# Causal attention: the last norm's statistics of one sequence moved behind the last row maximum, and the copies of each group's outputs moved from VectorE to ScalarE

## The reference, cut to what matters

```python
h = _layernorm(x, ln1_w, ln1_b)          # then a causal convolution of three taps over the rows
q, k, v = jnp.split(h @ attn_w, 3, axis=-1)   # 16 heads of 8, rotated
scores = jnp.where(causal, q @ k.T / jnp.sqrt(D), -1e30)
y = jax.nn.softmax(scores, axis=-1) @ v
x = x + y @ proj_w
h = _layernorm(x, ln2_w, ln2_b)
expert_idx = jnp.argmax(h @ router_w, axis=-1)     # one of 4 experts for each row
x = x + chosen expert of h (gate * sigmoid(gate) * value @ expert_proj)
```

## Time and profile before

| what | us |
|---|---|
| median of 3 runs | 343.56 (342.61 to 343.8) |
| the profiled execution | 344.2, its span 342.4 |
| TensorE, VectorE, ScalarE, GpSimd busy | 317.1, 248.9, 216.5, 127.7 |
| attention loop in the profile | about 107 to 187 |
| L900, the copies, 8 on VectorE | 119.4 to 186.9, 0.68 each |

### The profile page before, as it was taken

The page is one execution under the profiler, slowest core; times in us unless marked ns, Lnnn a source line. Parts: engine busy times, 40 slices in busy tenths (PEclk is TensorE's granted clock), DMA queues, the critical chain, the costliest instruction groups (busy, mean ns, idle before and its releaser), DMA issues.

```text
span 342.4 us, 6803 instructions
## 1 busy us (share of the span) xinstructions
PE 317.1 (93%) x2270; PEld 221.3 (65%) x2270; DVE 248.9 (73%) x766; ACT 216.5 (63%) x641; POOL 127.7 (37%) x183
## 2 busy tenths in 40 slices
PE   8799989998989999997999998998999899999886
PEld 2348778664544333354544998995678687878675
DVE  4988875884889999988352563379787867888476
ACT  1488885374466755564378664764776576676995
POOL 3455563110732444403231360410685525545400
PEclk9999999999999999998799999999999999999999
DMA  7590000086752520090002003100100000000002
GB/s 210 192 278 5 2 0 2 9 264 173 208 190 72 138 74 3 11 351 15 2 17 71 2 23 101 50 0 0 56 17 17 1 2 0 3 0 0 2 0 64
DMA packets 21881, 22.47 MB, mean 66 GB/s; under 512 B 3894, under 2 KB 18646, under 8 KB 21846
## 3 DMA queue, kind: packets, MB, share of 16 engines
q1 hardware_dynamic: 18982, 16.78, 17.0%
q10 hardware_dynamic: 2352, 4.20, 3.8%
q0 software_dynamic: 512, 1.05, 1.0%
HBM read 14.22 MB, written 7.60 MB: 64 GB/s over the span
## 4 chain that ended last, share of the span: by engine, by line
PE 57%; DVE 17%; ACT 13%; issue 5%; POOL 4%; DMA 3%; SPq 0%; ACTq 0%; POOLq 0%
PE PS L1388 51%; PE PS L1442 5%; DVE PS L873 5%; ACT big L1176 5%; ACT big L1364 3%; POOL big L529 2%; DVE big L691 2%; DMA big<-in_A_WkT 2%; DVE big L716 2%; ACT big L1306 1%; DMA XN<-scr_y,pos 1%; ACT big L1150 1%; DVE XN L668 1%; POOL big L531 1%; DVE mraw L705 1%
## 5 line engine op out<-in xcount | busy, mean ns | idle before, releaser
L1388 PE MATMUL PS<-big 128*128 128x128 f32 (+10 forms) x592 | 94.6, 311 | 9.1 <-DVE mB L873 4.1
L1388 PEld LDWEIGHTS PS<-big 128*128 128x128 f32 (+3 forms) x592 | 56.4, 151 | 42.9 <-DVE mB L873 21.3
L529 POOL TENSOR_TENSOR big<-big,urec 128x1024 f32<-128x1024 f32 x24 | 45.6, 1898 | 60.2 <-DVE urec L723 45.5
L1176 ACT ACTIVATE big<-big 128x154 f32<-128x154 f32 x192 | 60.5, 318 | 10.9 <-DVE big L691 5.6
L873 DVE CUSTOM_DVE_ANT_0 PS<-PS,later 128x128 f32<-128x128 f32 (+3 forms) x128 | 59.9, 516 | 8.8 <-PE PS L1388 7.6
L1306 ACT ACTIVATE big<-PS 128x1024 f32<-128x1024 f32 (+3 forms) x64 | 42.8, 701 | 31.1 <-PE PS L1388 31.1
L1150 ACT ACTIVATE big<-PS 128x1280 f32<-128x1280 f32 (+2 forms) x30 | 32.3, 1087 | 27.0 <-PE PS L1442 24.5
L1388 PE MATMUL PS<-kkC,XT 128*128 128x462 f32 (+1 forms) x96 | 36.0, 511 | 2.2 <-DVE big L716 2.2
L517 POOL TENSOR_TENSOR rstd<-ve,minus_half 128x4 f32<-128x4 f32 (+2 forms) x13 | 13.2, 1016 | 61.8 <-DVE ve L663 61.8
L1176 ACT ACTIVATION_READ_ACCUMULATOR big<-big 128x1 f32 x192 | 36.1, 188 | 0.0
L1388 PEld LDWEIGHTS PS<-vwCm,big 128*128 128x128 f32 x256 | 30.9, 192 | 3.9 <-ACT big L1150 1.3
(11 more groups left out here) (193 smaller groups left out, 507.0 us busy)
## 6 DMA issues: line engine op xcount, KB each, us to landing
scr_qk<-big SPq DMA_DIRECT2D x12, 384.0 KB, 3.3
big<-scr_qk SPq DMA_DIRECT2D x16, 288.0 KB
big<-in_wv ACTq DMA_DIRECT2D x1, 2048.0 KB, 8.0
scr_x<-zrow SPq DMA_DIRECT2D x2, 448.0 KB, 6.4
scr_y<-big SPq DMA_DIRECT2D x2, 448.0 KB, 3.5
X<-in_x ACTq DMA_DIRECT2D x2, 256.0 KB, 3.4
big<-in_A_WoT ACTq DMA_DIRECT2D x1, 512.0 KB, 4.7
cw<-in_C_Wk SPq DMA_DIRECT2D x1, 512.0 KB, 5.3
```

The source lines that it names most:

```text
L529: pool.tensor_tensor(pn[:, 0:GH * P].rearrange("p (h k) -> p h k", h=GH), Pt[u % 3][:, :, 0:KM], r.to_broadcast([P, GH, KM]), ALU.mult).th ...
L1176: i = act.activation(Pt[u % 3][:, h, :], Pt[u % 3][:, h, :], ACT.Exp, accum_out=usum[:, u % 3, h:h + 1])
L1388: return pe.matmul(o, lhsT, rhs, start=start, stop=stop)
```

## The change

Four edits. On VectorE, `ln_m(0)` moves from step 20 to step 22, behind the last three maxima; `add_attention(0)` stays in step 20. On GpSimd, `split_maxima(7)` moves from behind `apply_m(0)` to before the root of that norm. `copy_outputs` leaves VectorE, with its waits, and stands in ScalarE's loop before the first exponential of the same steps (5, 9, ... 29). The last one, `copy_outputs(1, 3)`, stands behind ScalarE's loop, before `slots_out`. What is computed is the same.

```diff
@@ GpSimd
             split_maxima(6)
+            split_maxima(7)
...
             for b in range(B):
                 ln_rsqrt("m", (b,))
                 apply_m(b)
-                if b == 0:
-                    split_maxima(7)
                 pool.wait_ge(ln_norm["m"], QT * b + QT)
                 scatter(b)
@@ VectorE
-            def copy_outputs(b, g):
-                dve.wait_ge(av_step, QT * (4 * b + g + 1))
-                if b:
-                    dve.wait_ge(y_turned, g + 1)
-                dve.tensor_copy(yg[:, g, :], PS[:, AV_BANK, :]).then_inc(yg_ready, 1)
-
...
             for s in range(2 * 16):
                 g = (s - 5) // QT
-                if s % QT == 1 and s >= 5:
-                    copy_outputs(*divmod(g, 4))
                 if s < M_STEPS:
                     ring_maximum(3 * s)
...
                 elif s == S_TAIL + 2:
                     add_attention(0)
+                elif s == M_STEPS:
                     ln_m(0)
                 elif s == S_TAIL + 5:
                     route(0)
...
-            copy_outputs(1, 3)
             normalise_group(1, 3)
@@ ScalarE
+            def copy_outputs(b, g):
+                act.wait_ge(av_step, QT * (4 * b + g + 1))
+                if b:
+                    act.wait_ge(y_turned, g + 1)
+                copy(yg[:, g, :], PS[:, AV_BANK, :]).then_inc(yg_ready, 1)
+
             for n in range(B * 4 * QT * 2):
                 s, pair = divmod(n, 2)
+                if not pair and s % QT == 1 and s >= 5:
+                    copy_outputs(*divmod((s - 5) // QT, 4))
                 w = T - P * (s % QT)
                 act.wait_ge(st_mm, n + 1)
...
+            copy_outputs(1, 3)
             for part in range(len(SLOT_PARTS)):
                 slots_out(0, part)
```

## The result

The changed kernel takes **340.18 us** in the median of 6 runs (339.01 to 340.81); the kernel before, beside it, takes 343.69 (342.61 to 344.07, 6 runs). The ratio is **0.9899**, 95% interval [0.9872, 0.9926]. Forecast were 338.6 and a range of 336.7 to 341.0. Faster was right and the range holds the time, but the gain is 3.5 us and not 5. All medians and ranges here are of all executions, while the ratios and their intervals leave out the few that lie 1.5% or more above the fastest of the same kernel. The profiled executions give 344.2 and 340.81, with spans of 342.35 and 338.63, so 3.7 us of the gain can be followed in the two traces.

The account below looks back on a forecast made before the run. TensorE was taken to bound the kernel, through its waits in the attention loop and a clock dip. Terms -0.45 - 5.0 + 0.05 + 0.45 = -4.95 took the profiled 344.2 to 339.25, median 338.6; range 336.7 to 341.0.

Parts of the forecast that it names:

- The statistics moved: Steps 20 to 22: VectorE takes the next maximum earlier, TensorE's 2.15 us stall goes and its clock stays full; gain 5.0.
- the ring: Steps 5, 9, 13, 17: without VectorE's copy, output products start when GpSimd's mask ends, 0.13 earlier; gain 0.45 in all.
- Rival (a): Attention loop: maxima, not TensorE's last product, set the group, so four copies give 2.4 instead of 0.45; 336.7, chance 0.10.
- Step 29: ScalarE's copy stands behind an expert's weight copy, so TensorE's output products start at 182.6 instead of 182.14; 0.45 lost.
- Rival (b): ScalarE's copies delay exponentials at three steps, or step 23's slack is overrun; 1.4 comes back, 340.0, chance 0.15.
- the slack of step 23: TensorE turns the last maxima at 165.4, the router's first operation is done at 164.8: 0.6 us of slack, cost 0.
- Rival (c): Step 21: the clock dips all the same, from another cause; only 2.1 gained, 341.5, chance 0.08.
- Rival (d): Step 23: TensorE waits for the router behind statistics and root, and its clock falls; 344.9 at 3 us waiting, chance 0.04.
- Step 25: ScalarE's copy stands behind the last exponential, and TensorE has scores to do before needing the bank; 0.05 lost.
- Rival (e): Nothing measurable: waits behind ScalarE's eight copies (8 x 0.47 = 3.8) eat the gain; 342.6, chance 0.03.

Follow-up runs that it names:

- the experiment with a busy TensorE: Kernel before, plus nine products of ones on TensorE during its wait in step 21, into a free bank: 340.69 us, ratio 0.9911.
- the copy twice: Changed kernel with the copy of step 29 done twice on ScalarE, to lengthen TensorE's wait: 342.11 us, ratio 0.9946.
- the change the third time: Changed kernel, unaltered, measured again on the third chip: 339.92 us, ratio 0.9898 to the kernel before.
- the change again: Changed kernel, unaltered, measured again on the second chip: 339.79 us, ratio 0.9894 to the kernel before.
- copy ahead, again: Changed kernel with each copy behind the previous step's last exponential, in step 28 ahead of the weight copy; second measurement, another chip: 340.11 us, ratio 0.9871.

## Why the prediction was right, and where it was not

**The statistics moved: right, in size and in place.** Forecast 5.0, measured 5.12. Its steps stand in the trace one by one: no stall in step 21, the router's products at 162.31 (162.9 less 0.45 for the ring was said), last maximum done at 161.1 (161.5 less 0.45), root from 162.58 (163.1 less 0.45), first operation of the router done at 164.27 (164.8 less 0.45), the turn at 164.82 (165.4 less 0.45, 164.95), with nobody waited for. (The changed trace reaches S 0.25 earlier, which these comparisons leave in.) The stall was 2.15 of the 5.0, which leaves 2.85 for the clock and the rest. By the experiment with a busy TensorE the clock is 2.66 of the 5.12 and the wait about 2.2.

**The ring: right in sign, mis-sized.** Forecast 0.45. S to A gives 0.23 in this pair of traces, but it differs by 0.30 between the three traces of the change. The starts of the output products are steadier: their distance over four steps is shorter by 0.03, 0.05, 0.06 and 0.06 up to those of steps 4, 8, 12 and 16, 0.20 together. Outside of dips all traces with the copies on VectorE have groups of 9.46, all with the copies on ScalarE 9.40. The step that failed: "Without VectorE's copy the mask decides, 0.13 earlier." The mask decided before as well. Its end and the start of the weight loads lie 0.25 apart in the kernel before (138.88 and 139.13) and 0.23 in the change (119.72 and 119.95, in step 5), and the bracket of the earlier trace rows names POOL. What the 0.06 comes from instead was not traced. A releaser that the profile names, and whose end fits the start, is better evidence than a difference of 0.13 between ends. Rival (a), 2.4 from the ring, is refuted by the same rows.

**Step 29: the wait right, the clock missed.** Forecast 0.5 from B to C (0.45 and 0.05); without a dip it is 16.97 in two traces against 16.30, so 0.67. The copy itself was priced well: "TensorE starts at 182.6" was 0.46 behind 182.14, and by the experiments the copy costs 0.54. The other 0.13 stays when that copy is back on VectorE (16.43 against 16.30). What has no term is the dip, 1.5 us in the profiled execution. I had asked of the clock what brings it down in step 21, and never what the added wait does to it in step 29: the term of 0.45 should have carried a second one with a chance of its own, 0 or 1.5. Rival (b) came out near the time (340.0), but by another mechanism: no exponential came late in the ring, and the slack of step 23 was not overrun.

**Sum.** -0.23 - 5.12 + 0.67 + 1.52 = -3.16 in the loop, and -0.56 in the two stretches outside. Without the dip of step 29, the change's traces have spans of 336.87 and 337.23, and those executions take 339.05 and 339.41: 0.5 to 0.8 above the forecast. But the dip explains the profiled execution and not the median. Five of the six timed runs of the change have a mean clock of 0.998 or more, which leaves no room for a dip, and they take 339.01 to 340.44. So of the 1.6 us between the forecast (338.6) and the median (340.18) the loop accounts for about 0.3 (4.68 gained without the dip, for 4.95). The rest lies in what moves from run to run at full clock, 338.72 to 341.01 for the change on the second chip, and stays open. That the time fell inside the range does not show that the loop was priced to the microsecond.

**Rival (c)** fell with the products of ones. But one argument against it was wrong: "the three timed runs lie within 1.2 us, less than a dip costs". Three runs were too few. Of the 15 runs of the kernel before on the second chip two are at 0.96 and 352; of the others the one with mean clock 1.0 takes 341.14, three at 0.994 or 0.995 take 342.90 to 343.18, six at 0.989 or 0.990 take 342.85 to 344.22, and three at 0.984 take 344.80 to 345.33. That is 3.9 us from the first to the mean of the last, over 0.016 of mean clock. The Trainium skill (TensorE: Matmul & The Clock Gate, Part 1) says that the moment at which the clock changes differs from run to run. The page gives this for the rise; the traces agree with it for the fall, which stands 0.25 us ahead of the end of the stall in the kernel before (160.5 and 160.76), 0.5 behind it with the copies alone (162.1 and 161.63), and 1.8 ahead of the end of the wait with the split left behind (167.9 and 169.70). The prediction had set it aside.

**Rival (d)** was priced at 2.7 us of waiting for a loss of 1 us. The experiment shows the mechanism with 4.16 of waiting, and its time lies 0.94% above the kernel before. At the rival's prices that wait costs 7.5 (4.16 and 3.3 for the clock); measured are 6.7 over the change without a dip (3.75, and 2.96 of the 4.48, leaving out step 29). Its chance stayed low for the right reason: the split of the maxima stands ahead of the root.

**Step 25: right against the kernel before.** Forecast 0.05 lost; the output products start 3.62 behind B, and 3.61 before. What the forecast had no term for is that its two halves hang together: with the statistics moved and the copy left on VectorE they start 4.12 behind.

**Rival (e)** has a slip in its sum: 8 x 0.47 = 3.8 less of 4.95 gained gives 342.4, not 342.6. It changes no chance.

## What to carry to other kernels

When work is moved away from a wait, price what TensorE's idle time does to the clock at both ends: here half of the gain from the statistics was the clock, and a new wait of half a microsecond stood ahead of a dip of 1.5 us in some executions. Where a wait can't be removed, a few useless products in a free bank keep the clock (nine of them saved 2.66 us). And for each step moved past a queue, ask what else in that queue now stands behind it. The maxima's split, left behind the norm, turned 1% gained into 1% lost.

## What the runs showed of the hardware

- One kind of cause gives dips of different lengths. Behind nearly the same stall (2.15 and 2.16) the dip was 6.8 us in one execution and 3.4 in another, and with the 4.16 of the split left behind it was 10.2. The fall stands 0.25 ahead of the end of the wait, 0.5 behind it and 1.8 ahead of it.
- The clock also fell where no single idle time is long. Ahead of the dip in step 29 the weight loads of the changed kernel have gaps of 0.62, 0.58 and 0.73 us. Six traces have the late copy and its wait: three show the dip (the change, copies alone, split left behind), three do not (the change twice more, and the copy twice, with a gap of 1.22). So what decides between the two is not known. The six traces without the late copy show none there, nor does the one with products of ones in the wait.
- Near 110 us, early in the loop, six of the thirteen traces show a dip. It begins ahead of step 5, the first step that any edit touches. It costs about 0.8 to 1.7 us (S to A 57.8 to 58.5 against 56.7 to 57.0), and 8 us in the one trace where it is 20.5 us long.
- Behind C, where the code of all variants is the same but for the last copy, the traces spread from 154.7 to 157.6, one kernel two or three times within 0.8. Two places make the spread. At one and the same weight load about 76 us behind C the four traces of the first chip are 1.3 us or more later than the nine others (76.8 to 76.9 against 75.4 to 75.5), whatever their edits. And 3 to 4 us behind that load TensorE's idle time ahead of one weight load of the second layer is anything from under 0.05 (the change the third time, 154.72, the shortest) over 0.53 (the change again) to 1.12 (the statistics moved alone, 157.56, the longest) and 1.30 (copy ahead, again). What makes that wait longer or shorter is open. So differences of half a microsecond are read from stretches here and not from the whole time.
